# A transformer block on one core: halved softmax steps, folded biases, two small jobs moved to ScalarE, and a new slot table

## What is computed

```
q = (x @ Wq.T + bq).reshape(B, S, H, Dh)         # H = 16 heads, Dh = 8
v = (x @ Wv.T + bv).reshape(B, S, H, Dh)
bits = (einsum('bshe,en->bshn', [q, 1], hyperplanes) >= 0)   # 6 bits: a bucket of 64
scores = einsum('bhsd,bhtd->bhst', q, q) / sqrt(E)
attn = softmax(scores * (62 + (bucket_s == bucket_t)), axis=-1)
att = einsum('bhst,bhtd->bhsd', attn, v)
x = x + layernorm(att(layernorm(x)))
h = silu(x1 @ w1.T * w1_s) * (x1 @ w2.T * w2_s)   # x1 = layernorm(x), 512 wide
h = gelu(h @ h1.T * h1_s);  h = gelu(h @ h2.T * h2_s)
x = x + layernorm(h @ w3.T * w3_s)
```

## Time and profile before

| | |
|---|---|
| median of 3 runs | 1373.44 us (1372.72 to 1375.92) |
| the profiled execution | 1380.13 us, of which the span from first to last instruction 1378.3 us |
| busy share of the span | PE 89%, DVE 89%, POOL 85%, ACT 79% |
| mean granted TensorE clock | 0.975 of full |

### The profile page before, as it was taken

One profiled execution on the slowest core, in us unless ns is written; L12 is line 12 of the kernel. 1 busy time (PEld: TensorE's weight loads), 2 busy tenths in 40 slices (PEclk: granted clock), 3 DMA queues, 4 the chain that ended last, 5 costly groups with the idle time before them and its releaser, 6 DMA issues. The chain is left out here.

```text
span 1378.3 us, 19705 instructions
## 1 busy us (share of the span) xinstructions
PE 1230.9 (89%) x5402; PEld 502.9 (36%) x5402; DVE 1222.5 (89%) x3838; ACT 1082.2 (79%) x1605; POOL 1167.3 (85%) x164
## 2 busy tenths in 40 slices
PE   4766799999989999998999899998989999998997
PEld 1211234334343433433343433434343343433343
DVE  4988999989999999999999999999999999999420
ACT  2344778879797988979698897979788897969875
POOL 1699889898989989899998989899898989999800
PEclk9877999999999999999999999999999999999999
DMA  4473445445544455454545535444454445543100
GB/s 105 149 186 112 118 124 147 125 122 122 143 121 129 131 136 133 116 145 120 129 115 146 134 111 139 134 129 122 128 147 119 129 122 129 136 125 100 62 5 11
DMA packets 89470, 167.37 MB, mean 121 GB/s; under 512 B 18192, under 2 KB 54160, under 8 KB 89360
## 3 DMA queue, kind: packets, MB, share of 16 engines
q1 hardware_dynamic: 89252, 165.82, 44.7%
q10 hardware_dynamic: 108, 0.30, 0.1%
HBM read 150.59 MB, written 15.47 MB: 120 GB/s over the span
## 5 line engine op out<-in xcount | busy, mean ns | idle before, releaser
L991 POOL TENSOR_TENSOR logits<-max_row,logits 128x4096 f32<-128x4096 f32 x128 | 1139.0, 8914 | 109.0 <-DMA max_row<-max_scratch 67.0
L826 DVE CUSTOM_DVE_ANT_0 logits<-s_bank,coeff 128x512 f32<-128x512 f32 x1024 | 693.6, 677 | 0.0
L1040 ACT ACTIVATE logits<-logits 128x1024 f32<-128x1024 f32 x512 | 503.0, 1046 | 81.5 <-POOL logits L991 81.2
L776 DVE TENSOR_SCALAR coeff<-brow,bcol 128x516 bf16<-128x516 bf16 x1024 | 488.1, 477 | 47.0 <-PE s_bank L560 45.1
L560 PE MATMUL s_bank<-mov_stack,stat_stack 128*128 128x512 bf16 x1024 | 348.5, 394 | 51.1 <-DVE rowmax L826 44.2
L580 PE MATMUL aux_bank<-logits,v_pad 128*32 128x512 f32 x2048 | 254.7, 617 | 34.1 <-ACT logits L1040 33.8
L715 PE MATMUL f_bank<-hid_b,h_sb 128*128 128x512 f32 x512 | 247.2, 596 | 1.3 <-ACT hid_b L1170 1.2
L704 PE MATMUL f_bank<-hid_a,h_sb 128*128 128x512 f32 x512 | 243.8, 592 | 0.0
L560 PEld LDWEIGHTS s_bank<-mov_stack,stat_stack 128*128 128x128 bf16 x1024 | 94.5, 98 | 359.1 <-DVE rowmax L826 228.0
L715 PEld LDWEIGHTS f_bank<-hid_b,h_sb 128*128 128x128 f32 x512 | 96.6, 191 | 85.6 <-issue 71.0
L704 PEld LDWEIGHTS f_bank<-hid_a,h_sb 128*128 128x128 f32 x512 | 95.0, 190 | 85.7 <-issue 77.6
(11 more groups left out here) (112 smaller groups left out, 927.7 us busy)
## 6 DMA issues: line engine op xcount, KB each, us to landing
max_row<-max_scratch SPq DMA_DIRECT2D x128, 512.0 KB, 4.1
brow<-bucket_scratch SPq DMA_DIRECT2D x63, 522.0 KB, 6.7
mov_stack<-q_scratch SPq DMA_DIRECT2D x192, 96.0 KB
stat_stack<-q_scratch SPq DMA_DIRECT2D x189, 96.0 KB
max_scratch<-rowmax_T SPq DMA_DIRECT2D x512, 1.0 KB
q_scratch<-q_parts SPq DMA_DIRECT2D x16, 384.0 KB, 4.6
x_in<-in_x SPq DMA_DIRECT2D x16, 256.0 KB, 3.1
q_scratch<-q_parts SPq DMA_DIRECT2D x16, 256.0 KB, 5.1
```

The lines of the kernel that those rows point to most:

```text
L776: nc.vector.tensor_scalar(coeff[:, k % 3, :].rearrange("p (r n) -> p r n", r=ROW_RUNS), brow[:, h // 4 % 2, h % 4, :, 0:RUN], bcol[:, b % ...
L826: nc.vector.tensor_tensor_reduce(out=logits[:, ring(b, k), :], in0=tile_bank(k)[:], in1=coeff[:, k % 3, 0:SEQ], scale=float(E) ** -0.5, sc ...
L991: nc.gpsimd.tensor_tensor(tiles, max_row[:, m % 2].unsqueeze(2).broadcast_to([P, GROUP, ST, SEQ]), tiles, ALU.subtract).then_inc(below_max ...
L1040: nc.scalar.activation(logits[:, first:first + 2, :], logits[:, first:first + 2, :], ACT.Exp, scale=-1.0).then_inc(probs_done, 1)
```

## The change

Six things, all shown below. (1) POOL subtracts in two halves per group: row blocks 0 and 1 of both heads, then 2 and 3. The four exponentials follow the halves, and step j = 0 of the value product waits for all of the first group but only the first half of the second; step j = 2 waits for the rest. (2) bq and bv become rows of 128 that are added by two short matmuls into the centred weights (each weight column is raised by bias/128); xnT gets 1.0 added, and since the rows of x are now centred by a bias of their own, the product yields the bias. For that ACT makes x_shift = -mean, POOL x_bias = x_shift times rstd, and the normalization uses x_bias. (3) The three additions of bq fall away; DVE's q step becomes a plain subtraction. (4) The copy of the values into v_pad goes from DVE to ACT. (5) The reciprocals go from DVE to ACT, as exp(-ln(sum)), two instructions of 128x32. (6) Nearly all slots are new.

```diff
-COPY_LAG = 35
-DIVIDE_LAGS = (40, 40)
+COPY_LAG = 37
+RDEN_LAG = 37
+DIVIDE_LAG = 40
-XNT_COPY_SLOT = 54
-XNT_SLOT = 58
-Q_SLOT = 61
+XNT_COPY_SLOT = 53
+XNT_SLOT = 60
+Q_SLOT = 63
-V_ADD_SLOT = 32
+V_ADD_SLOT = 29
-SUB_SLOT = 14
-EXP_SLOTS = (13, 14, 14, 15)
+SUB_SLOT = 11
+EXP_SLOTS = (13, 13, 14, 14)
...
-            for n, weights in enumerate((wq_sb, wv_sb)):
-                nc.tensor.matmul(f_bank[n][:, 0:E], centre, weights[:], start=True, stop=True).then_inc(centred_psum, 1)
+            for n, (weights, shift) in enumerate(((wq_sb, bq_sb), (wv_sb, bv_sb))):
+                nc.tensor.matmul(f_bank[n][:, 0:E], centre, weights[:], start=True, stop=False)
+                nc.tensor.matmul(f_bank[n][:, 0:E], even_row[:], shift[:], start=False, stop=True).then_inc(centred_psum, 1)
...
+                    pe.wait_ge(probs_done, b * (TILES // 2) + (quad + 1) * QT // 2 - GROUP)
+                if j == 2:
                     pe.wait_ge(probs_done, b * (TILES // 2) + (quad + 1) * QT // 2)
...
-                    nc.vector.reciprocal(rden[:].unsqueeze(3), o8[:, :, :, DH:DH + 1]).then_inc(rden_done, 1)
...
-                nc.gpsimd.tensor_tensor(tiles, max_row[:, m % 2].unsqueeze(2).broadcast_to([P, GROUP, ST, SEQ]), tiles,
-                                        ALU.subtract).then_inc(below_max_done, 1)
+                for t in (0, 2):
+                    nc.gpsimd.tensor_tensor(tiles[:, :, t:t + 2],
+                                            max_row[:, m % 2].unsqueeze(2).broadcast_to([P, GROUP, 2, SEQ]),
+                                            tiles[:, :, t:t + 2], ALU.subtract).then_inc(below_max_done, 1)
...
-                act.wait_ge(below_max_done, b * GROUPS + m + 1)
-                first = ring(b, m * GT) + 2 * n
+                act.wait_ge(below_max_done, 2 * (b * GROUPS + m) + n // 2 + 1)
+                first = ring(b, m * GT) + ST * (n % 2) + n // 2 * 2
...
+            def invert_sums(b, pair):
+                sums = aux_bank[:].rearrange("p (t h w) -> p t h w", t=ST, w=HALF_W)[:, :, :, DH:DH + 1]
+                done = b * PAIRS + pair
+                act.wait_ge(o_psum, done + 1)
+                nc.scalar.activation(den_log[:].unsqueeze(3), sums, ACT.Ln).then_inc(den_log_done, 1)
+                act.wait_ge(den_log_done, done + 1)
+                if done:
+                    act.wait_ge(att_done, done)
+                nc.scalar.activation(rden[:], den_log[:], ACT.Exp, scale=-1.0).then_inc(rden_done, 1)
...
+            def project_step(p, k):
+                if k == V_ADD_SLOT:
+                    act.wait_ge(v_psum, p + 1)
...
+                    nc.scalar.copy(
+                        v_pad[:, p % 2, :, 0:PAD_PITCH - HALF_W].rearrange("p r (h w) -> p r h w", w=VW)[:, :, :, 0:DH],
+                        projection_bank(p, 1)[:].rearrange("p (r h d) -> p r h d", r=2 * ST, d=DH)).then_inc(v_added, 1)
```

More of the change, by code:

```diff
@@ L195, in sandwich_kernel @@
         x_rstd = sb("x_rstd", [P, ST])
+        x_shift = sb("x_shift", [P, ST])
+        x_bias = sb("x_bias", [P, ST])
         xnT = sb("xnT", [P, SEQ])
@@ L954, in iteration @@
                         transpose_maxima(i - 1, GROUPS - 1)
[L955 to L957 removed]
+                    for b, pair in pairs_at(i, k, DIVIDE_LAG, attend, feed):
+                        output_step(b, pair)
                     if project:
@@ L1010, in iteration @@
                         nc.gpsimd.tensor_tensor(ffn[:], ffn[:], y1[:, g % 2], ALU.add).then_inc(y2_done, 1)
+                    if query and k == x_slot(i + 2, X_BIAS_SLOT, LATE_X_BIAS_SLOT):
+                        pool.wait_ge(x_shift_done, i + 3)
+                        pool.wait_ge(x_rstd_done, i + 3)
+                        nc.gpsimd.tensor_tensor(x_bias[:], x_shift[:], x_rstd[:], ALU.mult).then_inc(x_bias_done, 1)
                 if query and not project:
@@ L1072, in query_step @@
                         act.wait_ge(v_psum, p)
-                    nc.scalar.copy(xnT[:], aux_bank[:]).then_inc(xnT_done, 1)
+                    nc.scalar.activation(xnT[:], aux_bank[:], ACT.Identity, bias=1.0).then_inc(xnT_done, 1)
                 if k == Q_HIGH_SLOT:
@@ L1192, in iteration @@
                         copy_output(b, pair)
+                    for b, pair in pairs_at(i, k, RDEN_LAG, attend, feed):
+                        invert_sums(b, pair)
                     if project:
```

169 lines of the change are left out of this document (83 added, 86 removed).

## The result

| | before | after |
|---|---|---|
| median | 1374.68 us (1372.72 to 1376.69) | 1353.71 us (1353.54 to 1355.77) |
| ratio to before | | 0.9851, 95% interval 0.9832 to 0.987 |
| the profiled execution | 1380.13 us | 1353.54 us |

The account below looks back on a forecast made before the run. DVE's work plus its stalls was taken as the batch; 28.1 us from the steady batches and the other stages summed to 40.2, from 1380.13 to 1339.9, and 6.7 off for the profiled execution gave 1333 us (range 1314 to 1356).

Parts of the forecast that it names:

- What bounds the kernel: Steady batches 3 to 13: DVE's queue, 75.92 us of work plus 3.42 idle, makes the batch of 79.35 us.
- The stretch: ACT from output copy to end of ynT: 26.0 us before, 26.1 after, so part of DVE's gain returns as waiting.
- The number 76.8: Steady batch in us, taken between 76.0 and 77.5: 2.55 less a batch, 28.1 us over 11 batches.
- The halves: PE's wait for exponentials ahead of the value product, 1.9 us a batch, should be gone with POOL's halved subtraction.
- The moved steps: Reciprocals 0.78, value addition 0.61 and q bias 0.06 leave DVE: 1.45 us a batch, its work falling to 74.47.
- The table: New slots: about 2 us less PE work in slots 0 to 10, about 1 us more in 32 to 39.
- POOL: Eight extra instructions at 0.1 us each and x_bias at most 0.2: 73.5 us of work a batch.
- The port lock: Each of eight more POOL starts costs a coefficient instruction, some 0.5 us: 1342 us; chance counted within another rival's 0.22.
- The waits named: Steady part: none of PE for exponentials or DVE for rden; DVE's for att_bias and PE's for ynT unchanged or larger.
- the slower rival: The query chain, its product two slots later, makes DVE wait at its q subtraction: up to 1393 us, chance 0.09.
- only DVE's own work goes: Rival: DVE loses 1.45 us a batch while its stalls stay at 3.4: 1347 us, chance 0.22.
- The other stages: Gains: batch 0 0.7 us, batches 1 and 2 3, 14 and 15 4, after the last scores 4.4; start costs some tenths.

Follow-up runs that it names:

- act_less_out: The changed kernel with two exponentials of the seventh group, outside ACT's stretch from output copy to ynT, cut to 64 of 512 columns: 1359.42 us, ratio 0.9877.

## Why the forecast had the direction and half the size

**What bounds the kernel: the step that failed.** "DVE's queue is the longest, so its work plus its stalls is the batch" is true as bookkeeping and wrong as a cause. It makes every microsecond taken off DVE a gain unless a wait grows; but the waits are not a property of DVE. With the halves in, a batch is 25.4 us in which ACT works without a gap and the others wait for it, and 52.5 us from ynT to the next output copy, of which DVE's work is one part among others. The forecast took 1.45 us a batch from DVE (measured 1.29); the idle time of DVE fell by 0.32 where the sum had 1.1.

**The stretch.** It was read and priced rightly: 26.0 us before and 26.1 forecast (to the end of ynT), and 26.4 in batch 7; the means from start to start are 25.56 and 25.61. One term was missing, ACT's wait for POOL behind the output copy (0.55 a batch). The wait for the transposes, forecast 0.7, is 0.75, the inverse 0.43 for 0.5, the copy 0.57 for 0.6. The consequence was drawn too weakly. "Part of what DVE gains there will be given back in waiting" should have been all of it inside the stretch, since ACT's stretch kept its length. The number 76.8, "between them, for the ynT stretch", had no working behind it, and it is the term that missed: 2.55 us a batch forecast, 1.62 measured, 10.3 us over 11 batches.

**The halves.** The mechanism was right: PE's wait for exponentials, 21.0 us in the steady part, is gone, and the halves alone give the whole gain. Its size was not. The wait was 1.9 us a batch and was taken as one sum; but half of it (1.09) stood inside the stretch, where the batch waits for ACT in any case, and only the other half (0.96) outside. The rest fell from 53.57 to 52.51, 1.06 us, the stretch by 0.21.

**The moved steps.** Forecast as a gain of 1.45 us of DVE. The runs show 7 and 15 us of loss with the old table, and with the new one no difference that can be told: 0.9857 with the halves and the table, 0.9851 with all. The stretch is only 0.48 longer there, since the inverse lies in ACT's wait for POOL, and the rest is 0.55 shorter. Under the old table the rest did not shrink by the moves. Under the new one it is 52.42 with the reciprocals alone back on DVE, but also 52.36 in act_less_out, which only takes work away; so whether DVE's smaller work gives those 0.5 us wasn't settled.

**The table.** Forecast at nothing but smaller clumps. It is worth nothing to the halves alone, costs 4.5% without them, and gives back 23 us with them and the moved steps, chiefly by taking two exponentials out of the stretch (27.07 to 25.61: 1.94 less, 0.55 back as the wait for POOL).

**POOL.** 73.5 us of work forecast, 73.85 measured. The extra starts cost 0.14 us for 0.1, and x_bias 0.21. The halved subtraction takes 4557 ns, the bound named being 4.55. The port lock did not happen, by the result as by the earlier trace rows: each of the eight further POOL starts cost 0.14 us, not the 0.5 us of a coefficient instruction. The Trainium skill, "SBUF — State Buffer" (section "SBUF: two separate sides"), speaks of VectorE instructions in a two-port mode; no run here shows in which mode the coefficient instruction runs. So this is no evidence against the rule, only that these two instructions don't hold each other up.

**The waits named.** DVE's wait for att_bias, forecast to stay or grow, is gone in the steady part (7.4 us before). DVE waits for rden once, after the last scores, where nothing else is left for it. At the q subtraction DVE has no wait in the steady part, so the slower rival did not come. The waits for ynT stayed, as said. The rival "only DVE's own work goes" named 1347 and comes nearest by number, but for the wrong reason: the halves, which leave DVE all its work, give as much.

**The other stages.** Batches 0 to 2 gave 6.0 us for 3.7, 14 and 15 gave 2.4 for 4, the filling cost 1.0. After the last scores 1.4 came for 4.4. The value products end earlier as forecast. PE's timeline of that stage:

```profile
1285.07 1.92 PE L593 MATMUL aux_bank<-logits,v_pad 128*32 128x512 f32 x16 [0.55 <-ACT logits L1037]
...
1306.01 1.98 PE L689 MATMUL f_bank<-ynT,w_sb 128*128 128x512 f32 x4 [0.91 <-ACT hid_a L1187]
1307.83 1.02 PE L703 MATMUL f_bank<-ynT,w_sb 128*128 128x512 f32 x2
1309.69 1.98 PE L703 MATMUL f_bank<-ynT,w_sb 128*128 128x512 f32 x4 [0.84 <-DVE hid_a L920]
```

The output copy comes 22.8 us after the last tile instead of 26.0 (1287.06 against 1315.42). But the new order of gate and up products leaves PE waiting for ACT and DVE twice more in the last feed-forward part. The halves with the old table have a last stage of 85.0 us, 3.9 less than before: there the forecast term (4.4) nearly came in.

**The median.** The sum was made against the profiled execution and 6.7 us taken off at the end. That execution was simply a long one; after's stood 0.2 below its median. Of the 20.7 us between 1333 and 1353.7, 13.6 are in the trace (40.2 forecast, 26.6 measured) and 6.9 are this.

## What to carry to other kernels

Where three in-order queues are over 90% busy, the longest need not be the pace. Look for the stretch in which one engine has no gap and the others wait at its end, whatever that engine's share, and write a batch as that stretch plus the rest. A step that moves into a stretch without a gap costs its full length, and one that leaves another engine there gives nothing. If the engine stands waiting somewhere in the stretch, a step put there costs only what the wait doesn't take up. Split a wait by where it stands before pricing its removal: inside the stretch of another engine it is worth little (here 0.21 of 1.09 us at most). A stretch is shortened by order before it is by work: what is ready ahead of the copy that is waited for goes behind it, but what is put ahead of the stretch must be ready when its turn comes, or its wait becomes the stretch. Moves and tables are tried together, since each can look worthless alone.

## What the runs showed of the hardware

- Of the 25.8 us of the changed kernel's stretch in batch 7, four loads of ACT's function tables take 5.1 (1.28 us each). The next activation starts at once: the load of 601.39 ends at 602.67, and the GELU starts at 602.69.
- In the changed kernel a logarithm of 128x32 from PSUM takes 0.197 us on ACT and an exponential 0.229 (means of 32 each), each less than DVE's reciprocal of the same shape (0.35 in the earlier trace rows), together more. What makes them dear under the old table is the wait for the transposes (0.75), which the reciprocal, standing later in DVE's queue, did not have.
- A subtraction on POOL of twice 2048 columns instead of 4096 costs 0.14 us more per extra instruction ((808.89 - 797.01)/88, halves against before), beside a DVE that is busy for 97% of that window.
